# Mamba phase on one Trainium2 core: y summed by accumulating fp32 transposes, skip on TensorE, gate on VectorE

## The reference

```python
xz = einsum('bld,ed->ble', x, in_w);  xb, z = split(xz, 2)
xb = silu(conv4(xb) + cb)
delta, Bm, Cm = split(einsum('ble,re->blr', xb, xp_w))
delta = softplus(einsum('blr,er->ble', delta, dtw) + dtb)
dA = exp(delta[..., None] * -exp(a_log))
mi = delta[..., None] * Bm * xb[..., None]
v = BETA * v + mi_t          # scan over time, per channel and state
h = dA_t * h + v
y_t = einsum('ben,bn->be', h, C_t)
y = y + dp * xb              # skip
y = y * silu(z)              # gate
out = einsum('ble,de->bld', y, ow)
```

## Time and profile before

| | us |
|---|---|
| time, median of 3 runs | 4441.87 (4441.69 to 4448.29) |
| span of the profiled execution | 4448.6 |
| TensorE busy | 3574.1 (80%) |
| VectorE busy | 2793.3 (63%) |
| GpSimd busy | 2081.9 (47%) |
| ScalarE busy | 1980.3 (45%) |

### The profile page before, as it was taken

One profiled execution on the slowest core, in us unless ns is written; L12 is line 12 of the kernel. 1 busy time (PEld: TensorE's weight loads), 2 busy tenths in 40 slices (PEclk: granted clock), 3 DMA queues, 4 the chain that ended last, 5 costly groups with the idle time before them and its releaser, 6 DMA issues. The chain is left out here.

```text
span 4448.6 us, 88475 instructions
## 1 busy us (share of the span) xinstructions
PE 3574.1 (80%) x28540; PEld 2392.4 (54%) x28541; DVE 2793.3 (63%) x4863; ACT 1980.3 (45%) x4454; POOL 2081.9 (47%) x1206
## 2 busy tenths in 40 slices
PE   6888869936988889888875888888988884499980
PEld 4454546624555555555543555555555553388870
DVE  3444432345777777777755777777777776655545
ACT  1212112205656666566634666656666553233320
POOL 0101000014667666676652766667667675422216
PEclk8888878967999999999986999999999995599995
DMA  1000000011313222132221221312223224211113
GB/s 50 0 0 0 0 21 0 0 56 41 74 51 73 52 54 74 49 75 52 53 63 33 64 61 51 76 50 60 66 51 73 51 55 152 99 48 47 47 40 109
DMA packets 151619, 230.36 MB, mean 52 GB/s; under 512 B 25106, under 2 KB 83890, under 8 KB 149556
## 3 DMA queue, kind: packets, MB, share of 16 engines
q1 hardware_dynamic: 143156, 202.30, 17.1%
q0 software_dynamic: 8064, 23.08, 1.8%
HBM read 119.99 MB, written 23.59 MB: 32 GB/s over the span
## 5 line engine op out<-in xcount | busy, mean ns | idle before, releaser
L893 POOL TENSOR_TENSOR m_hc<-m_h,m_Cb 128x1024 f32<-128x1024 f32 x512 | 1204.9, 2354 | 766.3 <-DVE m_h L1014 446.9
L1014 DVE TENSOR_TENSOR_SCAN m_h<-m_dA,m_hlast,m_bank 128x256 f32<-128x256 f32 x2048 | 1354.3, 725 | 145.3 <-PE m_bank L1295 62.6
L1277 PE MATMUL m_bank<-m_hc,ident 128*128 128x512 f32 x2048 | 1210.2, 680 | 147.9 <-POOL m_hc L893 147.6
L1144 ACT ACTIVATE m_dA<-m_delta,m_rate 128x256 f32<-128x256 f32 x2048 | 894.1, 500 | 16.3 <-DVE m_h L1014 15.4
L1293 PEld LDWEIGHTS m_bank<-m_M,m_U 128*128 128x128 bf16 x8192 | 605.1, 101 | 362.4 <-DVE m_h L1014 223.8
L1293 PE MATMUL m_bank<-m_M,m_U 128*128 128x64 bf16 x8192 | 675.2, 197 | 128.5 <-DVE m_h L1014 118.8
L1295 PEld LDWEIGHTS m_bank<-m_M,m_U 112*128 112x128 bf16 x8192 | 578.5, 100 | 205.6 <-issue 173.3
L1295 PE MATMUL m_bank<-m_M,m_U 112*128 112x64 bf16 x8192 | 675.3, 197 | 0.0
L1277 PEld LDWEIGHTS m_bank<-m_hc,ident 128*128 128x128 f32 x2048 | 337.8, 205 | 197.0 <-POOL m_hc L893 164.5
L962 DVE SCALAR_TENSOR_TENSOR m_cv<-m_xpre,m_conv,m_cv 128x256 f32<-128x256 f32 x384 | 272.3, 750 | 22.7 <-ACT m_cv L1082 18.2
L1207 PE MATMUL m_bank<-m_pair,m_in 128*128 128x256 f32 x1024 | 267.7, 388 | 7.6 <-ACT m_cv L1082 3.8
(11 more groups left out here) (273 smaller groups left out, 5637.6 us busy)
## 6 DMA issues: line engine op xcount, KB each, us to landing
m_Cb<-m_c_rows SPq DMA_DIRECT2D x256, 256.0 KB, 3.2
m_M<-m_Mhi SPq DMA_DIRECT2D x128, 256.0 KB, 4.1
m_M<-m_Mlo SPq DMA_DIRECT2D x64, 256.0 KB, 3.9
m_U<-m_Uhi SPq DMA_DIRECT2D x128, 128.0 KB, 3.2
y_rows<-x_y SPq DMA_DIRECT2D x40, 256.0 KB, 2.1
m_U<-m_Ulo SPq DMA_DIRECT2D x64, 128.0 KB, 3.4
g_stage<-in_e_w SPq DMA_DIRECT2D x8, 1024.0 KB, 5.4
o_stage<-in_e_w SPq DMA_DIRECT2D x16, 512.0 KB, 4.7
```

Of the source, the lines that this page charges most:

```text
L893: nc.gpsimd.tensor_tensor(hc[:, n % 2], h[:, n % RING], Cb[:, g % 2, n % NG, :].unsqueeze(1).broadcast_to([P, KI, CM]), ALU.mult).then_inc ...
L1014: nc.vector.tensor_tensor_scan(h[:, n % RING, m, :], dA[:, n % RING, m, :], VB[(n % 2) * 2 + g][:, (m % 2) * CM:(m % 2 + 1) * CM], hlast[: ...
L1144: nc.scalar.activation(dA[:, n % RING, m, :], delta[:, par, m, :], ACT.Exp, scale=rate[:, m, n:n + 1]).then_inc(s["da_done"], 1)
L1277: last = nc.tensor.matmul(Y[half][:], net.ident[:], hc[:, n % 2, 2 * half:2 * half + 2, :], start=(n == 0), stop=(n == NS - 1))
```

## The change

1. y is summed with time in the partitions. `accumulate` no longer multiplies by the identity; it puts each 128 x 128 block of hc in as the weights and transposes it into Y[j] (j = half of the chunk's time, channels in the free dimension), with accumulation: four transposes per half, eight per state.
2. The skip goes to TensorE: `skipped(c)` in slot 5 opens both banks with eight matmuls, xb as weights and a diagonal matrix `dskip` (built once per layer by four VectorE instructions) as moving operand.
3. The z half of the input projection is computed with time in the partitions too: xT as weights, 512 columns of w_in, the same number of column passes.
4. The gate is two VectorE instructions, zs = Y * zs (L995), in place of four for the skip and one on GpSimd. The first starts when the first half is summed (`sum_done`).
5. To go on, the gated y must have channels in partitions again: TensorE transposes it back into Y (L1275, eight transposes, slot 4), ScalarE copies it to u (L1139, two copies, slot 5), then the output projection runs as before.
6. xb has one buffer where it had two; its SiLU waits for `skip_done`. The SiLU of z waits for `gT_psum`, no longer for the gate on GpSimd.

```diff
-        xb, zs, delta = (sb(t, [P, 2, KI, CM]) for t in ("xb", "zs", "delta"))
+        xb, zs, delta = sb("xb", [P, KI, CM]), sb("zs", [P, 2, TM, DI]), sb("delta", [P, 2, KI, CM])
+        dskip = sb("dskip", [P, KI, P])
...
-                def tail(t, par, at):
-                    if at == 3:
-                        pool.wait_ge(s["gate_done"], 1 + t * KI + KI)
-                        pool.sem_inc(net.carrier, 1)
-                        nc.gpsimd.tensor_tensor(u[:], u[:], zs[:, par], ALU.mult).then_inc(s["gated_done"], 1)
...
+                for m in range(KI):
+                    nc.vector.scalar_tensor_tensor(dskip[:, m, :], net.ident[:], skip[:, m:m + 1], net.ident[:],
+                                                   ALU.mult, ALU.mult)
...
-                        dve.wait_ge(s["acc_done"], 1 + AHEAD + t * NS)
-                        for m in range(KI):
-                            nc.vector.scalar_tensor_tensor(u[:, m, :], xb[:, par, m, :], skip[:, m:m + 1],
-                                                           halves(Y[m // 2])[:, m % 2, :],
-                                                           ALU.mult, ALU.add).then_inc(s["gate_done"], 1)
+                        for j in range(TM):
+                            if j < TM - 1:
+                                dve.wait_ge(s["sum_done"], 1 + t)
+                            else:
+                                dve.wait_ge(s["acc_done"], 1 + AHEAD + t * NS)
+                            nc.vector.tensor_tensor(zs[:, par, j, :], Y[j][:], zs[:, par, j, :], ALU.mult
+                                                    ).then_inc(s["gate_done"], 1)
...
-                        act.wait_ge(s["gated_done"], 1 + q)
-                        for g in range(2):
-                            act.wait_ge(s["in_psum"], 1 + q * 4 + g + 3)
-                            nc.scalar.activation(zs[:, par, 2 * g:2 * g + 2, :], halves((H0, H1)[g]), ACT.Silu
+                        for j in range(TM):
+                            act.wait_ge(s["gT_psum"], 1 + q * TM)
+                            act.wait_ge(s["in_psum"], 1 + q * 4 + j + 3)
+                            nc.scalar.activation(zs[:, par, j, :], (H0, H1)[j][:], ACT.Silu
                                                  ).then_inc(s["z_done"], 1)
                         act.wait_ge(s["conv_done"], 1 + q * 2 + 2)
-                        nc.scalar.activation(xb[:, par], cv[:], ACT.Silu).then_inc(s["xb_done"], 1)
+                        act.wait_ge(s["skip_done"], 1 + q)
+                        nc.scalar.activation(xb[:], cv[:], ACT.Silu).then_inc(s["xb_done"], 1)
...
+                def tail(t, at):
+                    if at == 5:
+                        for j in range(TM):
+                            act.wait_ge(s["gT_psum"], 1 + t * TM + j + 1)
+                            nc.scalar.copy(u[:, :, j * P:(j + 1) * P], Y[j][:].rearrange("p (m t) -> p m t", t=P)
+                                           ).then_inc(s["gT_done"], 1)
...
+                            j, k = g - 2, m % 2
+                            last = nc.tensor.matmul((H0, H1)[j][:], xT[:, k, j * P:(j + 1) * P], w_in[:, k, DI:2 * DI],
                                                     start=(k == 0), stop=(k == KD - 1))
...
+                    if at == 4:
+                        for j in range(TM):
+                            pe.wait_ge(s["gate_done"], 1 + t * TM + j + 1)
+                            pe.sem_inc(net.carrier, 1)
+                            for m in range(KI):
+                                last = nc.tensor.transpose(Y[j][:, m * P:(m + 1) * P],
+                                                           zs[:, par, j, m * P:(m + 1) * P], net.ident[:])
+                            last.then_inc(s["gT_psum"], 1)
...
+                def skipped(c):
+                    for j in range(TM):
+                        pe.wait_ge(s["gT_done"], 1 + c * TM + j + 1)
+                        for m in range(KI):
+                            last = nc.tensor.matmul(Y[j][:, m * P:(m + 1) * P], xb[:, m, j * P:(j + 1) * P],
+                                                    dskip[:, m, :], start=(m == 0), stop=False)
+                    last.then_inc(s["skip_done"], 1)
...
-                    last = nc.tensor.matmul(Y[half][:], net.ident[:], hc[:, n % 2, 2 * half:2 * half + 2, :],
-                                            start=(n == 0), stop=(n == NS - 1))
+                    for m in range(KI):
+                        last = nc.tensor.matmul(Y[half][:, m * P:(m + 1) * P], hc[:, n % NHC, m, half * P:(half + 1) * P],
+                                                net.ident[:], is_transpose=True, start=False,
+                                                stop=(n == NS - 1 and m == KI - 1))
                     if half == 1:
                         last.then_inc(s["acc_done"], 1)
+                    elif n == NS - 1:
+                        last.then_inc(s["sum_done"], 1)
```

More of the change, by code:

```diff
@@ L656 @@
 BETA = 0.6
-RING, LEAD, OFF, NG = 4, 2, 10, 2
+RING, LEAD, OFF, NG, NHC = 4, 2, 10, 2, 2
 def mamba_phase(net, layer, xm):
@@ L692, in mamba_phase @@
         hlast = sb("hlast", [P, NS, KI])
-        hc = sb("hc", [P, 2, KI, CM])
+        hc = sb("hc", [P, NHC, KI, CM])
         Cb = sb("Cb", [P, 2, NG, CM])
@@ L706, in mamba_phase @@
                  "mf_done mhi_done mlo_done halo_done carry_psum chi_done clo_done moved_next moved "
[L707 removed]
+                 "v_psum da_done scan_done hlast_done hc_done acc_done y_psum sum_done gT_psum gT_done skip_done "
+                 "out_psum xm_done rate_done "
                  "floor_done const_done c_kept c_spread0 c_spread1").split()
@@ L828, in _ @@
                 nc.gpsimd.memset(hc[:, 0], 0.0)
-                for t in (xb, zs):
-                    last = nc.gpsimd.memset(t[:, 1], 0.0)
-                last.then_inc(s["setup"], 1)
+                nc.gpsimd.memset(zs[:, 1], 0.0).then_inc(s["setup"], 1)
                 pool.wait_ge(s["setup"], 1 + 1)
@@ L903, in slots @@
                         for at in (2 * n, 2 * n + 1):
-                            tail(c, 1 - par, at)
                             if more:
@@ L922, in _ @@
                 product(NCM - 1, 1, NS - 1, 0)
-                tail(NCM, 1, 3)
             @block.vector
@@ L1160, in slots @@
                                 keep_last(c, n - 1)
+                            tail(c, at)
                             if more:
@@ L1178, in _ @@
                 slots(NCM - 1, 1, False, False)
+                tail(NCM, 5)
             @block.tensor
@@ L1205, in head @@
                             pe.wait_ge(s["pre_done"], 1 + q * 2 + g - 1)
-                        for k in range(KD):
-                            last = nc.tensor.matmul((H0, H1)[g % 2][:, m % 2 * CM:(m % 2 + 1) * CM],
-                                                    w_in[:, k, m * P:(m + 1) * P], xT[:, k, :],
+                        if g < 2:
+                            for k in range(KD):
+                                last = nc.tensor.matmul((H0, H1)[g][:, m % 2 * CM:(m % 2 + 1) * CM],
+                                                        w_in[:, k, m * P:(m + 1) * P], xT[:, k, :],
+                                                        start=(k == 0), stop=(k == KD - 1))
+                        else:
+                            j, k = g - 2, m % 2
+                            last = nc.tensor.matmul((H0, H1)[j][:], xT[:, k, j * P:(j + 1) * P], w_in[:, k, DI:2 * DI],
                                                     start=(k == 0), stop=(k == KD - 1))
@@ L1215, in head @@
                         for k in range(KI):
-                            last = nc.tensor.matmul(H0[0:RANK + 2 * NS, 0:CM], w_xp[:, k, :], xb[:, par, k, :],
+                            last = nc.tensor.matmul(H0[0:RANK + 2 * NS, 0:CM], w_xp[:, k, :], xb[:, k, :],
                                                     start=(k == 0), stop=(k == KI - 1))
@@ L1315, in slots @@
                                 late(c, 1, 1)
+                            if at == 5:
+                                skipped(c)
+                                accumulate(c, 0, 0)
+                                accumulate(c, 0, 1)
                             elif n > 2:
                                 accumulate(c, n - 2, g)
-                            elif at == 5:
-                                accumulate(c, 0, 0)
-                                accumulate(c, 0, 1)
                             tail(c, 1 - par, at, more)
@@ L1342, in _ @@
                     late(NCM, n, 1)
+                tail(NCM, 1, 4, False)
                 tail(NCM, 1, 7, False)
```

12 lines of the change are left out of this document (5 added, 7 removed).

## The result

The changed kernel takes **4193.5 us** (median of 4 runs, 4182.4 to 4201.9) beside 4445.1 for the kernel before on the same chip: a ratio of 0.9425, 95% interval 0.9402 to 0.9448. It is faster by 252 us where 285 were forecast, and lies 36 us above the predicted 4157.

The account below looks back on a forecast made before the run. TensorE's ordered queue was taken to bound some stretches and full VectorE the others, neither a whole chunk. Terms sum to 9.2 us per chunk, 285 us over 31 chunks, off 4441.9: 4157 us, range 4020 to 4370.

Parts of the forecast that it names:

- Accumulation: TensorE: each half falls from 0.94 to 0.43 us, 16.3 us of TensorE over 32 halves per chunk.
- a sign of being wrong: The prediction called itself wrong if an accumulating transpose on TensorE cost more than 0.107 us.
- (b): VectorE's 6.84 us wait for the output projection before the residual: 2.4 us less per chunk (-4.6 to 3.2).
- (c): VectorE's 1.60 us wait at L970, the step size: 1.3 us less per chunk (0 to 1.6).
- (d): VectorE's waits of 1.21 and 1.98 us (Ulo and clo): 1.2 of 3.2 us less per chunk (0 to 2.0).
- (a): Stretch 1600 to 1624, VectorE's late scans: of 3.3 us idle, 2.5 us less per chunk (0 to 3.3).
- (e): VectorE's 2.00 us wait per chunk behind ScalarE's logarithm: stays, no gain.
- the convolutions: VectorE, freed of GpSimd's gate: second convolution from 4.80 towards 2.69, 2.1 us less per chunk; first, 0.4 less.
- Gate: VectorE: four instructions of 1.65 us become two of 1.38 in all, 0.3 us less per chunk.
- Skip: TensorE: eight added matmuls, 2.0 us per chunk, covered by the second convolution, so cost 0.
- Clock: TensorE with less work has more half-clock gaps: 1.0 us lost per chunk beyond what (b) holds.
- The rival with the clock at half: Transposes don't hold TensorE's full clock; at a share of 0.75 at half clock, 4615 us; chance 0.09.

Follow-up runs that it names:

- e3: Changed kernel with the accumulation as an ordinary fp32 matmul by the identity instead of a transpose, same place and layout: 4357.2 us, ratio 0.9793.
- e1: Changed kernel with SyncE issuing the transfers of u ahead of those of the matrix's low half: 4170.0 us, ratio 0.9378.
- e5: e1 with the carry's transfers also moved ahead of the chunk's last spread of C in SyncE's order: 4142.9 us, ratio 0.9321.
- e9: e1 with four buffers for C in place of two, and only the first channel block's skip diagonal, used for all four: 4198.4 us, ratio 0.9432.
- e12: e5 with half of each GpSimd product of h and C, two of four channel blocks left out of y: 4036.9 us, ratio 0.9079.
- e6: e5 with six of the skip's eight matmuls left out: 4161.2 us, ratio 0.9358.
- e8: e5 with all eight of the skip's matmuls issued twice: 4175.3 us, ratio 0.9382.
- e7: e5 with four buffers for C in place of two, and only the first channel block's skip diagonal, used for all four: 4196.1 us, ratio 0.9429.
- e10: e5 with GpSimd's next product waiting until VectorE's softplus operation and the first operation behind it are over: 4156.4 us, ratio 0.9344.
- e11: Changed kernel with GpSimd's next product waiting until VectorE's softplus operation and the first operation behind it are over: 4209.8 us, ratio 0.9469.

## Why the prediction was right, and where it was not

- **Accumulation.** Taken at 0.43 us a half, measured 0.47 (1569.11 to 1569.58), 0.94 before. Accumulating costs the transpose little or nothing. Right, though at 0.117 us a transpose it is just over the 0.107 that the prediction named as a sign of being wrong; 0.04 a half is about 1.3 us of TensorE per chunk.
- **(b), (c), (d).** Right in mechanism, and by e3 from the cause given, but for Ulo's part of (d), which hardly moved. (b) was taken too small: 101 us came of 74 forecast. In the chunk shown the wait is 3.89, against 4 to 5, and the granted clock is 1.00 from 1567.6 to 1605.1, over the whole chain; the forecast had its first three pieces at half clock. The prediction's "its first 4.0 at half clock" reads the chain before too long as well: the earlier trace rows have 0.50 from 1632.90 to 1636.20 and 1.00 up to 1632.80. Its sum doesn't use the 4.0.
- **(a)** is the step that failed: "The 3.3 us go, except where a scan still waits for its bank". TensorE did become shorter there, but `velocity` of the next chunk's first state was now due sooner than SyncE could bring the carry. The forecast looked at what TensorE and VectorE do in this stretch and not at the DMA queue, which has its own order. e1 and e5 show the wait shrink with the place in this queue (80.5 us, then 69.6 and 40.2); e9 shows that the nine issues by themselves leave a part of it. They do not show the 78 us come: in e5 the scans, busy and waiting, are 34 us better than before the change (1465.5 against 1499.6). A second part is GpSimd's products, for which TensorE waits longer than before, with `velocity` behind it; e12 gives 15 us more (1450.4), with GpSimd's load halved. Where the rest of the 78 is, no run shows.
- **(e) and the convolutions.** The second convolution did as forecast (2.70); the first gained 0.24 of the 0.4 taken (4.32 for 4.56). "VectorE's operation with both tensors in SBUF stands still for as long as GpSimd runs" was applied to the convolution alone. The series (1.39 to 2.67 us on average) and the softplus operation (2.04 to 2.49) are of the same kind, and with TensorE faster GpSimd's products fell on them: 55.4 us lost, of which 41.0 lie in time that was a wait for the logarithm. So that wait did not stay at 2.0 a chunk, as forecast, but shows as 0.59 in the chunk, with VectorE standing in the series instead.
- **Gate.** 0.3 us a chunk was the instructions alone. The wait of the four old ones for the accumulation (39.4) shrank to 14.6 as well; a term left out, in the change's favour.
- **Skip.** Cost 0 is borne out as far as e6 goes, which gained nothing by leaving six of the eight out; eight take 1.86 us (1577.91 to 1579.77), 2.0 was taken.
- **Clock.** The rival with the clock at half did not come. In the Mamba blocks the half clock covers 589 of 2451 us, before 510 of 2707 (sums of the clock records): more, as forecast, but a quarter of the time and not three quarters. The Trainium skill, "TensorE: Matmul & The Clock Gate", Part 4, states that the full clock doesn't engage for transposes. In the window 1540.30 to 1543.60 TensorE's stream is `velocity` and accumulating transposes alone, busy for 3.30 of 3.30 us at 0.50, and from 1543.7 on the clock is 1.00; so it came back behind this mix, and the row doesn't tell whether the transposes did their part or `velocity` alone. In e3, with ordinary matmuls in their place, half clock covers 333 of 2610 us; TensorE also has more work there, so the run doesn't tell the rule from the load.

The sum was nearer than its terms, and that was partly luck: (a) missed by 88 us, the convolutions by 15 and (e) by 14; (b) and the gate gave 56 more than taken, and the 31 set aside for the clock were part of these misses already.

What stays open: why e8 and e6 both lost through the softplus operation and the residual. That a softplus operation starts 0.01 us behind GpSimd's product in e7 and 0.07 ahead of it in e5 suggests that small shifts decide who goes first; no run isolates it. Open too is what the rest of (a) waits for, and why e7 and e9 lost: the softplus row is the largest that grew, but e10 and e11 show that taking this collision away need not give the time back.

## What to carry to other kernels

When a faster engine pulls a stretch together, ask of each operand when its DMA was issued and what stands ahead of it in that queue: here two groups of transfers moved in SyncE's order were worth 50 us, on top of the change's 252. A collision between two engines is not removed with the one instruction that shows it; list all instructions of that kind, and expect them to meet somewhere else. Making the second engine wait took the collision away here, but moved the loss to other waits (e11); less work on it (e12) took it from the softplus operation and the convolutions, though not from the series.
